# P divided by its row sums, and split into f16 halves, in two parts of eight heads each

## The chip, the cores and the metric

The kernel runs on one core of a Trainium2 chip. The metric is device time in microseconds for one execution. A core has five engines that run their own instruction streams and meet only at semaphores: TensorE (PE; its weight loads are shown as PEld), VectorE (DVE), ScalarE (ACT), GpSimd (POOL) and SyncE (SP, which here only issues DMAs). Within an engine instructions go in order.

## What is computed

The reference takes x, 64 batches of 64 positions by 512, and a condition of 64 by 512, and applies four residual layers one after the other: attention with a condition-dependent normalization, a linear resampling of the channels at places given by the condition, a GRU over the 64 positions and a coupled oscillator over the same positions. The change touches the first alone:

```python
xn = _rms_norm(x, g_norm) * (1.0 + scale) + shift      # scale, shift from the condition
q, k, v = split(xn @ W_qkv)                             # 16 heads of 32
q, k = _rms_norm(q, g_q), _rms_norm(k, g_k)
logits = einsum('bhqd,bhkd->bhqk', q, k) * 32 ** -0.5
attn = softmax(logits, axis=-1)
o = einsum('bhqk,bhkd->bhqd', attn, v)                  # heads joined to 512
x = x + o + o @ W_out
```

## The kernel before

The kernel has two stages. `recurrences` (GRU and oscillator, 64 steps in order) takes the time from about 640 us on and is not touched. `attention_and_sampling` fills the first 640 us. It works on pairs of batches: a pair is 2 x 64 = 128 tokens, one per partition, and there are 32 pairs, n = 0 to 31. The last four have the names N3, N2, N1 and N0.

The order of the work is written out by hand as a software pipeline. Each engine has a function `slot(pair, i)`, called for i = 0 to 30, in which `pair(d)` is the pair i + d. Pair i is projected in slot i (`project`, L1163), its scores and its softmax come in slot i + 1, `mix` (attention times V, L1241), the output projection (`proj`, L1253) and the residual in slot i + 2, and the resampling (`sample`, L1205) in slot i + 3. Since every engine takes its list in order, a late operation holds all that is behind it on its engine. The last pairs are written out after the loop.

All large products are made of f16 halves: a value is kept as its f16 rounding ("high") and the rest ("low"), and three products of halves are added. So for P (the attention weights) of pair p, with all 16 heads in `S` (128 x 1024, f32), the steps are, before:

- ScalarE, `exps`: 16 exponentials of 64 columns, one per head, each also summing its row into a column of `den` (two ahead of `high_o`, fourteen behind `guess`). For pairs 0 and 1, and for the last two, one Exp of the whole and a sum on VectorE take their place.
- VectorE, `invert_sum` (L860): the reciprocal of `den`, 128 x 16.
- POOL, `norm_p` (L432): `S` times it, 128 x 1024 in one instruction.
- ScalarE, `high_halves`: `S` to f16, last in its slot, behind `high_v` (V's high part) and `high_wr` (a piece of the weights of the GRU).
- POOL, `low_halves` (L437): the rest, to f16.
- SP, `turn_p` (L317): one transposing DMA takes both halves to `PT`, which `mix` reads in the next slot. It is the first entry in SP's slot. Behind it stand the load of x for three pairs on (L285), and the loads of `rows` (L289) and others.

For the last two pairs (N1, N0) TensorE turns P (`turn_p`, L1173), and there are no halves on POOL.

Around it, in a slot:

- VectorE, in order: `scale_x` (L779, waits for `keep_rs` on ScalarE), a one-hot build of 128 x 512 f16 (`build`, L795), `low_qk` (L771 and L774, which release `scores`, L1187), three builds, `sums_qk` (L817), `least` (L841), `sums_qk`, `means` (L804, writes `ms`), two builds, `low_o` (L881, writes the low part of `oT`, for which `proj` waits), `newton` (L809, L811, L813), `scale_qk` (L824), two builds, `invert_sum` (L860), `residual` (L888), `low_v` (L830), `weigh_taps` (L863), `low_wr` (L909, in slots 4 to 27), `weigh_taps`.
- POOL, in order: `modulate` of the next pair (L453, two instructions, waits for `scale_x`), `add_taps` twice (L425, L428), `low_x1` (L447, two), `low_x` (L460), `norm_p`, `low_halves`.
- TensorE, in order: `turn_qk` (L1141), `project` 0, `scores`, `project` 1, `mix`, `project` 2, `proj`, `sample`, `turn_x` (L1262, L1264).

At the end of slot 3 VectorE also makes some seeds (`seeds`, L983 to L988). Nearly all activations go through one helper and have its line, L515, in the profile.

Of the kernel before, what the change touches and what calls it, by code (L numbers as in the profile page):

```python
# [5 lines left out]
ALU = mybir.AluOpType  # L6
# [99 lines left out]
def attention_and_sampling(nc, sems, ctx, block, banks, S_, x2_done, x2_first, ts_, first4, XR, condT, ident, Wx, later, x, cond, W_emb, b_emb, g_norm,  # L106
# [23 lines left out]
    def sem(name):  # L130
        return sems.enter_context(nc.semaphore(name))
# [110 lines left out]
    wr_in = [sem(f"wr_in{k}") for k in range(2)]  # L242
    ph_done, pl_done, pt_in = sem("ph_done"), sem("pl_done"), sem("pt_in")
    wih_out = [sem(f"wih_out{u}") for u in range(2)]
# [37 lines left out]
    def _(sp):  # L282
# [31 lines left out]
        def turn_p(p):  # L314
            sp.wait_ge(pl_done, p.n + 1)
            need(sp, mix_done, p.n)
            sp.dma_start_transpose(PT[:, :, :, :].rearrange("p i j n -> p (i j) n"), halves.rearrange("p i s k -> p (i s k)"))\  # L317
                .then_inc(pt_in, 16)
# [64 lines left out]
    def _(pool):  # L383
# [46 lines left out]
        def norm_p(p):  # L430
            pool.wait_ge(rden_done, p.n + 1)
            nc.gpsimd.tensor_tensor(S[:, :, :], S[:, :, :], rden[:, :].unsqueeze(2).broadcast_to([PART, HEADS, T]), ALU.mult)\  # L432
                .then_inc(p_done, 1)

        def low_halves(p):
            pool.wait_ge(ph_done, p.n + 1)
            nc.gpsimd.tensor_tensor(halves[:, 1, :, :], S[:, :, :], halves[:, 0, :, :], ALU.subtract).then_inc(pl_done, 1)  # L437

# [74 lines left out]
    def _(act):  # L513
# [76 lines left out]

        def high_halves(p):
            act.wait_ge(p_done, p.n + 1)
            need(act, pt_in, p.n * 16)
            a(halves[:, 0, :, :], S[:, :, :]).then_inc(ph_done, 1)

# [5 lines left out]
        def exps(p, lo, hi):  # L601
            act.wait_ge(mn_done, p.n + 1)
            need(act, pl_done, p.n)
            for s in range(lo, hi):
                e = a(S[:, s, :], psB[:, s // 8, s % 8 * T:(s % 8 + 1) * T], ACT.Exp, scale=-1.0, bias=mn[:, s:s + 1],
                      accum_out=den[:, s:s + 1])
            if hi == HEADS:
                e.then_inc(exp_done, 1)
# [40 lines left out]
        def slot(pair, i):  # L649
# [36 lines left out]
            if p := pair(-1):  # L686
                if p.n > 1:
                    exps(p, 2, HEADS)
                else:
                    exps_at_once(p)  # L690
# [7 lines left out]
            if p := pair(-1):  # L698
                high_halves(p)

# [60 lines left out]
    def _(dve):  # L761
# [81 lines left out]
        def subtract_least(p):  # L843
            dve.wait_ge(mn_done, p.n + 1)
            if p.n == N0.n:
                dve.wait_ge(p_T, 1)
            else:
                need(dve, pl_done, p.n)
            v.tensor_tensor(S[:, :, :], psB[:, :, :].rearrange("p h (s k) -> p (h s) k", k=T),
                            mn[:, :].unsqueeze(2).broadcast_to([PART, HEADS, T]), ALU.subtract).then_inc(sub_done, 1)  # L850
# [5 lines left out]

        def invert_sum(p):
            dve.wait_ge(exp_done, p.n + 1)
            need(dve, p_done, p.n)
            v.reciprocal(rden[:, :], den[:, :]).then_inc(rden_done, 1)  # L860

# [128 lines left out]
        def slot(pair, i):  # L990
# [38 lines left out]
            if i == 0:  # L1029
                low_cp(0)  # L1030
            if tap:
                build(tap, 1, (2, 3))
            if p := pair(-1):
                if p.n < 2:
                    sum_p(p)
                invert_sum(p)
            if p := pair(-2):
# [57 lines left out]
        sum_p(N1)  # L1095
        invert_sum(N1)
        residual(N2)
# [6 lines left out]
        sum_p(N0)  # L1104
        invert_sum(N0)
        low_o(N1)
# [23 lines left out]
    def _(pe):  # L1130
# [36 lines left out]
        def turn_p(p):  # L1167
            pe.wait_ge(p_done, p.n + 1)
            need(pe, qk_ready, NP)
# [723 lines left out]
```

## Time and profile before

| | us |
|---|---|
| median of three runs | 1564.39 (1557.45 to 1566.65) |
| the profiled execution | 1563.98 |
| its span, first to last instruction | 1562.2 |
| steady slots of the first stage, from 107.45 to 545.40 | 437.95 |
| busy in the span: TensorE, VectorE, ScalarE, POOL | 1497.6, 1363.3, 942.4, 750.1 |

Times in rows are from the span's start. L12 is line 12 of the kernel before. A row of a timeline gives start, duration, engine, line, operation, output and inputs by the program's names, shape, count and, in brackets, how long the engine had been idle before and what released it; a tile shown as `front`, `room`, `first` or `x` can be another buffer laid over it (`halves` lies in `front`, the one-hot matrices in `room`).

### The profile page before, as it was taken

To read this page: it belongs to the slowest core of one execution; us is meant where nothing else is said; L and a number is where in the kernel's file an instruction comes from. 1 tells how busy PE (TensorE), PEld (TensorE's weight loads), DVE (VectorE), ACT (ScalarE), POOL (GpSimd) and SP (SyncE) were. 2 spreads that over 40 slices of the span, in tenths; PEclk is the share of its full clock that TensorE was granted. 3 is DMA by queue.
4 is the path that set the end of the run, shared out by engine and by line. 5 is a ranking of instruction groups with operands and counts; after the bars stand their busy time and mean duration, and the time that the engine had idled before them with its cause. 6 is when DMAs were issued, how large, how long until landed. Compare 5 with 4: busy or idle time off the path is not lost.

```text
span 1562.2 us, 95585 instructions
## 1 busy us (share of the span) xinstructions
PE 1497.6 (96%) x42219; PEld 1327.1 (85%) x42219; DVE 1363.3 (87%) x3259; ACT 942.4 (60%) x2854; POOL 750.1 (48%) x887
## 2 busy tenths in 40 slices
PE   6899999999999999899999999999999999999995
PEld 3467776666667767899999999999999999999995
DVE  7889889888888889498888989988999889988997
ACT  6667777767777764355555555555555555555553
POOL 2566666666666665443433343433434343434331
PEclk8999999999999999999999999999999999999996
DMA  6333333444444434000000000000000000000000
GB/s 226 57 81 95 88 84 83 96 101 100 103 109 100 83 65 130 10 12 15 15 13 14 15 15 13 13 15 15 14 13 15 15 15 13 13 15 14 14 13 15
DMA packets 169054, 75.56 MB, mean 48 GB/s; under 512 B 139768, under 2 KB 154272, under 8 KB 168640
## 3 DMA queue, kind: packets, MB, share of 16 engines
q1 hardware_dynamic: 168544, 69.44, 19.4%
q8 instruction: 331, 5.42, 1.5%
q14 instruction: 83, 0.68, 0.1%
q10 hardware_dynamic: 96, 0.02, 0.0%
HBM read 33.71 MB, written 11.60 MB: 29 GB/s over the span
## 4 chain that ended last, share of the span: by engine, by line
PE 82%; DVE 5%; ACT 4%; issue 3%; POOL 3%; DMA 2%; ACTq 0%; POOLq 0%; DVEq 0%
PE psB L1472 34%; PE psA L1501 15%; PE psQ L1163 10%; PE psA L1506 7%; PE psQ L1205 6%; PE psO L1253 4%; DMA PT<-front 2%; ACT S L515 2%; PE psO L1241 2%; PE psB L1187 1%; PE psA L1141 1%; POOL S L432 1%; POOL front L437 1%; ACT front L515 1%; DVE room L795 1%
## 5 line engine op out<-in xcount | busy, mean ns | idle before, releaser
L1472 PE MATMUL psB<-first,Wx 128*128 128x64 f16 x9216 | 293.5, 194 | 5.5 <-POOL first L1784 3.8
L1501 PE MATMUL psA<-ts,Cp 128*128 128x64 f16 x8160 | 283.8, 194 | 10.3 <-ACT ts L1539 10.0
L1472 PE MATMUL psB<-first,Whh 128*128 128x64 f16 x9072 | 286.4, 193 | 0.8
L1472 PEld LDWEIGHTS psB<-first,Wx 128*128 128x128 f16 x9216 | 280.7, 98 | 6.7 <-POOL first L1784 3.9
L1163 PE MATMUL psQ<-Wx,front 128*128 128x512 f16 x1152 | 269.4, 384 | 6.3 <-DVE front L970 4.1
L1472 PEld LDWEIGHTS psB<-first,Whh 128*128 128x128 f16 x9072 | 273.8, 98 | 1.6 <-issue 1.6
L1539 ACT ACTIVATE ts<-qst 128x256 f16<-128x256 f32 x192 | 80.1, 417 | 313.9 <-DVE qst L1643 313.9
L1501 PEld LDWEIGHTS psA<-ts,Cp 128*128 128x128 f16 x8160 | 258.7, 99 | 11.5 <-ACT ts L1539 11.0
L1163 PEld LDWEIGHTS psQ<-Wx,front 128*128 128x128 f16 x1152 | 108.8, 99 | 126.7 <-issue 8.1
L1780 POOL TENSOR_TENSOR en<-rz,dn 128x256 f32<-128x256 f32 x64 | 46.8, 731 | 255.8 <-issue 255.6
L1506 PE MATMUL psA<-ts,Cp 128*128 128x64 f16 x4080 | 163.4, 194 | 0.7 <-issue 0.2
L795 DVE TENSOR_SCALAR room<-rows,lidx 128x512 f16<-128x512 f16 x256 | 158.0, 659 | 0.2 <-issue 0.2
L1506 PEld LDWEIGHTS psA<-ts,Cp 128*128 128x128 f16 x4080 | 138.6, 99 | 1.4 <-issue 1.2
L432 POOL TENSOR_TENSOR S<-S,rden 128x1024 f32<-128x1024 f32 x32 | 61.0, 1905 | 157.6 <-DVE rden L860 157.6
L1670 DVE TENSOR_TENSOR ts<-psA,ts 128x256 f16<-128x256 f32 x255 | 107.1, 420 | 31.7 <-ACT psA L1539 26.3
L515 ACT ACTIVATE S<-psB,mn 128x64 f32<-128x64 f32 x448 | 133.2, 338 | 0.6 <-DVE mn L841 0.4
L1643 DVE SCALAR_TENSOR_TENSOR rest<-cub,psQ 128x256 f32<-128x256 f32 x256 | 106.3, 415 | 7.0 <-DVE cub L1674 0.5
L1780 POOL TENSOR_TENSOR V<-X3b,first 128x256 f32<-128x256 f32 x64 | 47.0, 735 | 134.1 <-DVE first L1764 133.9
L1205 PE MATMUL psQ<-x,room 128*128 128x128 f16 x1856 | 108.5, 219 | 0.0
L1643 DVE SCALAR_TENSOR_TENSOR psO<-qst,psO 128x256 f32<-128x256 f32 x256 | 106.5, 416 | 0.0
L1205 PEld LDWEIGHTS psQ<-x,room 128*128 128x128 f16 x1856 | 104.9, 98 | 0.2
L515 ACT ACTIVATION_READ_ACCUMULATOR S<-psB,mn 128x1 f32 x448 | 104.0, 232 | 0.0
(201 smaller groups left out, 3001.0 us busy)
## 6 DMA issues: line engine op xcount, KB each, us to landing
front<-in_x SPq DMA_DIRECT2D x32, 256.0 KB, 4.6
rows<-rows_dram SPq DMA_DIRECT2D x64, 128.0 KB, 3.1
out<-ot SPq DMA_DIRECT2D x512, 16.0 KB, 1.8
x<-x SPq DMA_DIRECT2D x29, 224.0 KB
Whh<-in_L_cond_W_qkv SPq DMA_DIRECT2D x12, 256.0 KB, 7.2
room<-in_L_cond_W_hh SPq DMA_DIRECT2D x12, 256.0 KB, 2.7
room<-in_L_cond_W_ih SPq DMA_DIRECT2D x12, 256.0 KB, 2.8
wih_dram<-room SPq DMA_DIRECT2D x12, 256.0 KB, 3.2
```

What stands on the lines that cost most here:

```text
L432: nc.gpsimd.tensor_tensor(S[:, :, :], S[:, :, :], rden[:, :].unsqueeze(2).broadcast_to([PART, HEADS, T]), ALU.mult)\
L515: return nc.scalar.activation(out, in_, f, **k)
L795: e = v.tensor_scalar(E_of(p, b)[:, k, :], rows[b][:, :], lidx[:, k:k + 1], None, ALU.is_equal)
L1163: last = mm(psQ[:, n, :], xn[p.u][:, i, c, :], Wqkv[:, j, c, n * D:(n + 1) * D], start=(c == 0 and t == 0), stop=(c == KC - 1 and t == 2))
L1205: last = mm(o[:, m, :, :], E_of(p, b)[:, c, m * PART:(m + 1) * PART], x1_of(p)[:, :, i, c, b, :], start=(c == 0 and i == 0), stop=(c == KC ...
L1472: last = mm(o, W_[:, i, c, g * PART:(g + 1) * PART], src[:, j, c, :], start=False, stop=False, skip_group_check=True)
L1501: mm(psF[:, s % 2, m, :], Cp[:, i, c, m * PART:(m + 1) * PART], ts_[:, 0, c, :], start=(c == 0 and m == 0 and i == 0), stop=False, skip_gr ...
L1506: last = mm(psF[:, s % 2, m, :], Cp[:, 0, c, m * PART:(m + 1) * PART], ts_[:, 1, c, :], start=False, stop=(c == KC - 1), skip_group_check= ...
L1539: return nc.scalar.activation(out, in_, f, **k)
L1643: return v.scalar_tensor_tensor(out=flat(out), in0=flat(in0), scalar=scalar, in1=flat(in1), op0=ALU.mult, op1=op1)
L1670: v.tensor_tensor(ts_[:, 1, :, :], th, ts_[:, 0, :, :], ALU.subtract).then_inc(S["ts_ready"], 1)
L1780: return nc.gpsimd.tensor_tensor(flat(out), flat(in0), flat(in1), op)
```

## The change

P's division and its split are made in two parts, heads 0 to 7 and heads 8 to 15. The eighth exponential (s = 7) now signals `exp_half`. VectorE makes the first reciprocal (128 x 8) right after `scale_qk`, ahead of the last two builds, and the second where the whole one was. POOL multiplies the two parts in two instructions and then makes the two low parts in two. ScalarE makes the first high part after the sixteenth exponential and ahead of `high_v`, and the second at the end of the slot. The transposing DMA is one as before, and waits for both. For pairs 0 and 1 and for the last two, which have no exponentials by head, both parts start from the end of the whole, one after the other; `rden_done`, `p_done`, `ph_done` and `pl_done` count twice per pair, and all that waits for them is adjusted.

```diff
--- before.py
+++ after.py
@@ -240,7 +240,7 @@
     cp_in, wo_in, wo_plus, wo_hi, wo_lo, cT_done, cp_hi, cp_lo, wr_hi, wr_lo = (
         sem(n) for n in ("cp_in", "wo_in", "wo_plus", "wo_hi", "wo_lo", "cT_done", "cp_hi", "cp_lo", "wr_hi", "wr_lo"))
     wr_in = [sem(f"wr_in{k}") for k in range(2)]
-    ph_done, pl_done, pt_in = sem("ph_done"), sem("pl_done"), sem("pt_in")
+    ph_done, pl_done, pt_in, exp_half = sem("ph_done"), sem("pl_done"), sem("pt_in"), sem("exp_half")
     wih_out = [sem(f"wih_out{u}") for u in range(2)]
 
     def turned_coupling():
@@ -312,7 +312,7 @@
             sp.dma_start(stage[k % 2], wr_source(k)).then_inc(wr_in[k % 2], 16)
 
         def turn_p(p):
-            sp.wait_ge(pl_done, p.n + 1)
+            sp.wait_ge(pl_done, p.n * 2 + 2)
             need(sp, mix_done, p.n)
             sp.dma_start_transpose(PT[:, :, :, :].rearrange("p i j n -> p (i j) n"), halves.rearrange("p i s k -> p (i s k)"))\
                 .then_inc(pt_in, 16)
@@ -428,13 +428,16 @@
             nc.gpsimd.tensor_tensor(r, r, us, ALU.add).then_inc(x2_done, 1)
 
         def norm_p(p):
-            pool.wait_ge(rden_done, p.n + 1)
-            nc.gpsimd.tensor_tensor(S[:, :, :], S[:, :, :], rden[:, :].unsqueeze(2).broadcast_to([PART, HEADS, T]), ALU.mult)\
-                .then_inc(p_done, 1)
+            for h in range(2):
+                pool.wait_ge(rden_done, p.n * 2 + h + 1)
+                part = S[:, 8 * h:8 * h + 8, :]
+                nc.gpsimd.tensor_tensor(part, part, rden[:, 8 * h:8 * h + 8].unsqueeze(2).broadcast_to([PART, HEADS // 2, T]), ALU.mult)\
+                    .then_inc(p_done, 1)
 
         def low_halves(p):
-            pool.wait_ge(ph_done, p.n + 1)
-            nc.gpsimd.tensor_tensor(halves[:, 1, :, :], S[:, :, :], halves[:, 0, :, :], ALU.subtract).then_inc(pl_done, 1)
+            for h in range(2):
+                pool.wait_ge(ph_done, p.n * 2 + h + 1)
+                nc.gpsimd.tensor_tensor(halves[:, 1, 8 * h:8 * h + 8, :], S[:, 8 * h:8 * h + 8, :], halves[:, 0, 8 * h:8 * h + 8, :], ALU.subtract).then_inc(pl_done, 1)
 
         def low_x1(p):
             x1 = x1_of(p)
@@ -588,10 +591,10 @@
             need(act, mix_done, p.n - 1)
             a(Vt[p.u][:, 0, :], psQ[:, 2, :]).then_inc(v_hi, 1)
 
-        def high_halves(p):
-            act.wait_ge(p_done, p.n + 1)
+        def high_halves(p, h):
+            act.wait_ge(p_done, p.n * 2 + h + 1)
             need(act, pt_in, p.n * 16)
-            a(halves[:, 0, :, :], S[:, :, :]).then_inc(ph_done, 1)
+            a(halves[:, 0, 8 * h:8 * h + 8, :], S[:, 8 * h:8 * h + 8, :]).then_inc(ph_done, 1)
 
         def high_p(p, h):
             act.wait_ge(p_T, p.n - N2.n)
@@ -600,10 +603,12 @@
 
         def exps(p, lo, hi):
             act.wait_ge(mn_done, p.n + 1)
-            need(act, pl_done, p.n)
+            need(act, pl_done, p.n * 2)
             for s in range(lo, hi):
                 e = a(S[:, s, :], psB[:, s // 8, s % 8 * T:(s % 8 + 1) * T], ACT.Exp, scale=-1.0, bias=mn[:, s:s + 1],
                       accum_out=den[:, s:s + 1])
+                if s == HEADS // 2 - 1:
+                    e.then_inc(exp_half, 1)
             if hi == HEADS:
                 e.then_inc(exp_done, 1)
 
@@ -686,6 +691,7 @@
             if p := pair(-1):
                 if p.n > 1:
                     exps(p, 2, HEADS)
+                    high_halves(p, 0)
                 else:
                     exps_at_once(p)
             if i == 1:
@@ -696,7 +702,9 @@
             if 0 <= i - WR_FROM < WR_PIECES:
                 high_wr(i - WR_FROM)
             if p := pair(-1):
-                high_halves(p)
+                if p.n < 2:
+                    high_halves(p, 0)
+                high_halves(p, 1)
 
         act.wait_ge(cond_T, 1)
         a(condT[:, :, :], psC).then_inc(cond_kept, 1)
@@ -845,7 +853,7 @@
             if p.n == N0.n:
                 dve.wait_ge(p_T, 1)
             else:
-                need(dve, pl_done, p.n)
+                need(dve, pl_done, p.n * 2)
             v.tensor_tensor(S[:, :, :], psB[:, :, :].rearrange("p h (s k) -> p (h s) k", k=T),
                             mn[:, :].unsqueeze(2).broadcast_to([PART, HEADS, T]), ALU.subtract).then_inc(sub_done, 1)
 
@@ -854,10 +862,13 @@
             v.tensor_reduce(den[:, :], S[:, :, :], AX.X, ALU.add).then_inc(den_done, 1)
             dve.wait_ge(den_done, short(p))
 
-        def invert_sum(p):
-            dve.wait_ge(exp_done, p.n + 1)
-            need(dve, p_done, p.n)
-            v.reciprocal(rden[:, :], den[:, :]).then_inc(rden_done, 1)
+        def invert_sum(p, h):
+            if h == 0 and p.n in range(2, N1.n):
+                dve.wait_ge(exp_half, p.n - 1)
+            else:
+                dve.wait_ge(exp_done, p.n + 1)
+            need(dve, p_done, p.n * 2)
+            v.reciprocal(rden[:, 8 * h:8 * h + 8], den[:, 8 * h:8 * h + 8]).then_inc(rden_done, 1)
 
         def weigh(p, b, ts):
             return v.tensor_tensor(um[b][:, :, :, ts].rearrange("p c v t -> p (c v) t"),
@@ -1028,12 +1039,15 @@
             scale_qk(qk)
             if i == 0:
                 low_cp(0)
+            if (p := pair(-1)) and p.n > 1:
+                invert_sum(p, 0)
             if tap:
                 build(tap, 1, (2, 3))
             if p := pair(-1):
                 if p.n < 2:
                     sum_p(p)
-                invert_sum(p)
+                    invert_sum(p, 0)
+                invert_sum(p, 1)
             if p := pair(-2):
                 residual(p)
             low_v(qk)
@@ -1093,7 +1107,8 @@
         low_qk(N0, 0)
         low_qk(N0, 1)
         sum_p(N1)
-        invert_sum(N1)
+        invert_sum(N1, 0)
+        invert_sum(N1, 1)
         residual(N2)
         low_v(N0)
         least(N0)
@@ -1102,7 +1117,8 @@
         low_p(N1, 0)
         low_p(N1, 1)
         sum_p(N0)
-        invert_sum(N0)
+        invert_sum(N0, 0)
+        invert_sum(N0, 1)
         low_o(N1)
         weigh_taps(N3, 1)
         build(N2, 0, range(KC))
@@ -1165,7 +1181,7 @@
             last.then_inc(qkv_done, 1)
 
         def turn_p(p):
-            pe.wait_ge(p_done, p.n + 1)
+            pe.wait_ge(p_done, p.n * 2 + 2)
             need(pe, qk_ready, NP)
             if p.n == N0.n:
                 pe.wait_ge(pt_ready, 1)
```

## Rows read from the trace of the kernel before

**Rows 1.** The page: busy time of each engine, share of the span, instructions

```profile
PE 1497.6 (96%) x42219; PEld 1327.1 (85%) x42219; DVE 1363.3 (87%) x3259; ACT 942.4 (60%) x2854; POOL 750.1 (48%) x887
```

**Rows 2.** Windows: length, busy of each engine (instructions), granted clock, DMA, GB/s

```profile
107.45:545.40 437.95, 427.06 (x8474) 306.50 (x8473) 387.10 (x672) 324.10 (x1199) 290.58 (x265) 1.00 0.41 95
252.24:269.94 17.70, 17.60 (x356) 12.75 (x355) 15.00 (x29) 13.50 (x50) 11.27 (x11) 1.00 0.38 92
161.46:179.64 18.18, 17.76 (x356) 12.68 (x355) 16.98 (x29) 13.59 (x50) 12.81 (x12) 1.00 0.39 90
233.80:252.24 18.44, 17.97 (x355) 12.77 (x354) 17.40 (x29) 13.55 (x51) 12.94 (x12) 1.00 0.38 87
```

**Rows 3.** Waits of TensorE, 80 to 585 us: us in total, times, longest

```profile
PE psO L1241 <- DMA PT<-front: 3.8, 5, 1.0
PE psO L1241 <- issue: 1.9, 6, 0.6
PE psQ L1163 <- issue: 2.1, 2, 1.1
```

**Rows 4.** Timeline of TensorE, one slot: start us, us, instruction [idle before <-releaser]

```profile
165.01 0.97 PE L1187 MATMUL psB<-first 32*64 32x64 f16 x96
...
168.61 1.20 PE L1241 MATMUL psO<-PT,Vt 64*32 64x64 f16 x96
...
172.82 2.85 PE L1253 MATMUL psO<-oT,Wo 128*128 128x128 f16 x48 [0.32 <-DVE oT L881]
```

**Rows 5.** Timeline of VectorE and POOL, middle of the same slot

```profile
170.14 0.54 DVE L804 TENSOR_SCALAR ms<-ss 128x33 f32<-128x33 f32 x1
...
170.59 1.57 DVE L795 TENSOR_SCALAR room<-rows,lidx 128x512 f16<-128x512 f16 x2
...
169.04 1.59 POOL L447 TENSOR_TENSOR x<-XR,x 128x256 f16<-128x256 f32 x2
...
170.60 1.15 POOL L460 TENSOR_TENSOR front<-front 128x512 f16<-128x512 f32 x1
```

**Rows 6.** Timeline of POOL, starts of three slots

```profile
158.22 1.91 POOL L432 TENSOR_TENSOR S<-S,rden 128x1024 f32<-128x1024 f32 x1 [5.08 <-DVE rden L860]
161.29 2.14 POOL L437 TENSOR_TENSOR front<-S,front 128x1024 f16<-128x1024 f32 x1 [1.17 <-ACT front L515]
163.38 1.10 POOL L453 TENSOR_TENSOR front<-front,modA 128x512 f32<-128x512 f32 x1
...
236.01 1.10 POOL L453 TENSOR_TENSOR front<-front,modA 128x512 f32<-128x512 f32 x1
...
253.52 1.09 POOL L453 TENSOR_TENSOR front<-front,modA 128x512 f32<-128x512 f32 x1
```

**Rows 7.** Timeline of VectorE, both ends of the slot at 161.46

```profile
157.88 0.26 DVE L860 RECIPROCAL rden<-den 128x16 f32<-128x16 f32 x1 [1.19 <-ACT S L515]
...
160.42 0.69 DVE L909 SCALAR_TENSOR_TENSOR Whh<-room,Whh 128x512 f16<-128x512 f32 x1
...
161.97 0.69 DVE L779 TENSOR_TENSOR front<-psB,rsB 128x512 f32<-128x512 f32 x1 [0.17 <-ACT rsB L515]
...
173.36 1.29 DVE L824 TENSOR_TENSOR qn<-psQ,rs 128x512 f32<-128x512 f32 x2
...
175.39 0.25 DVE L860 RECIPROCAL rden<-den 128x16 f32<-128x16 f32 x1 [0.22 <-ACT S L515]
```

**Rows 8.** Groups of POOL, 80 to 585 us: count, busy us, mean ns

```profile
L453 POOL TENSOR_TENSOR front<-front,modB 128x512 f32<-128x512 f32 x27 | 28.3, 1049 | 2.1
```

**Rows 9.** Timeline of VectorE and POOL around 88 us

```profile
88.19 1.41 DVE L983 TENSOR_TENSOR brz<-vT 128x8 f32<-128x8 f32 x1
...
87.44 2.14 POOL L437 TENSOR_TENSOR front<-S,front 128x1024 f16<-128x1024 f32 x1 [1.17 <-ACT front L515]
```

**Rows 10.** Timeline of TensorE, the mix of pair 1

```profile
77.27 0.55 PE L1241 MATMUL psO<-PT,Vt 64*32 64x64 f16 x48 [1.58 <-DMA PT<-front]
```

**Rows 11.** The tile PT, 60 to 640 us: its DMAs from issue to landing

```profile
DMA to landing us min/median/max: 4.3/4.7/6.1
```

## What the change will do to the time

> **What bounds the kernel now.** I read the page first: TensorE is busy 96% of the span [rows 1]. The change touches the first 640 us only, so I cut the steady part of that stage into its slots (one slot per pair of batches). A slot starts with the transposes of q and k (L1141). From 107.45 to 545.40 us there are 24 (8474 matmuls at 356 in a slot), in 437.95 us, 18.25 each; TensorE is at full clock throughout. The slot at 252.24 took 17.70 us with TensorE busy for 17.60 of it: that is the floor. The slots at 161.46 and 233.80 took 18.18 and 18.44 [rows 2]. So all that the 24 slots hold above the floor is 437.95 - 24 x 17.70 = 13.2 us. Adding the slots before them, the change cannot be worth much over 15 us.
>
> The waits of TensorE between 80 and 585 us say what part is the transposing DMA: 3.8 us, in 5 slots of 28; 1.9 us stand in front of the same line with nothing named, 2.1 us inside the projections [rows 3]. The larger rest is short waits on VectorE, of which the one ahead of the output projection is seen in slot 161.46: L1253 waits there for `oT` (L881) [rows 4]. It comes 0.48 late, which is all of 18.18 less 17.70.
>
> Why is that wait there in one slot and not in the next? The middle of that slot answers it [rows 5]. One-hot builds (L795) and the small `ms` (L804) do not run while a POOL instruction runs: the `ms` at 170.14 ends 0.05 behind L447; the two builds at 170.59 end at 172.16, 0.41 after L460 (171.75), of which 0.15 is for the first and the rest for the second. Only then comes `low_o` (L881), and at 172.82 the output projection. So the time at which POOL starts its chain for the slot (modulate, L453) sets TensorE's loss at mid-slot: 163.38, 1.92 into the slot, gave 18.18, 1.28 gave 17.70, 2.21 gave 18.44 [rows 2, 6].
>
> **The change, part by part.** Times below are relative to the start of the following slot, here 179.64, the end of slot 161.46 (161.46 + 18.18). POOL's rows are [rows 6], VectorE's [rows 7].
>
> Sizes. Half a normalization is 128x512 f32 with one operand repeated along the row, the form of L453's second row: 1.05 us; half of the low parts has the form of L460, 1.15 to 1.16 us [rows 8, 5]. Two halves cost 2.10 and 2.32 against 1.91 and 2.14 whole, less 0.04 of overlap each: POOL works 0.3 us more in a slot of which it is busy for 12.81 of 18.18 [rows 2]. The copy of the whole to f16 on ScalarE fits between the end of L432 (160.13) and the start of L437 (161.29), 1.16 with two handovers of about 0.05. Half of it I take as 0.62, a little over the half, since a fixed part stays. The extra reciprocal is 0.25 on VectorE.
>
> 1. First reciprocal. It stands behind `scale_qk` (L824), which ends at 173.36 + 1.29 = 174.65, at -4.99. The eighth exponential is long done, so it ends at -4.80; POOL starts 0.08 later (158.14 to 158.22) and holds -4.75 to -3.70.
> 2. Today's reciprocal at 175.39 (-4.25) was released by ScalarE, so the last exponential ends at -4.3, and only the last two stand beside the first product. ScalarE then waits to -3.64 and copies to -3.02, and `Vt`'s high part ends at about -2.4 instead of -3.7. `low_v` on VectorE comes two residuals behind the second reciprocal, at -2.2: no cost. These are what is queued behind the new wait on ScalarE: `high_v`, then `high_wr`, which ends at -1.9, also before L909 wants it at -1.1; the second copy follows to -1.4.
> 3. The two builds that followed L824 now stand behind the first reciprocal. One starts before POOL, the other is held to -3.70 and ends at -3.55, 0.15 behind. The second reciprocal ends at R = -3.37. In this slot the single one ended at 175.64 = -4.00; in the slot before, at 158.14 = -3.32. The gap that VectorE had there is used up.
> 4. POOL then runs without a gap: second product to R + 1.13, first low part to R + 2.24, second low part R + 2.20 to R + 3.36 = 0.0. L437 used to end at 163.43, 1.97 into the slot. SP therefore issues the transposing DMA some 1.9 us earlier. Issue to landing is 6.1 us at most [rows 11]; `mix` starts at 168.61, 7.15 in [rows 4]: the 3.8 us of waits go. The load of x, behind it on SP, also goes out earlier; it is for three slots on, so worth nothing.
> 5. What it collides with. `low_wr` (L909, two operands in SBUF) starts 2.28 behind a reciprocal's end (160.42 - 158.14). Today POOL is idle there (L432 ended at 160.13, L437 starts at 161.29). Now the second low part has started 0.08 us before it. No row shows L909 against POOL. The nearest: L983, also two SBUF operands, of only 8 columns, took 1.41 us at 88.19, beside the L437 that ends at 89.58, and ended with it [rows 9]. So the bounds for L909's delay are 0 (it gets in first; a new neighbour on POOL cannot make it earlier) and 1.08 us (held from R + 2.28 to R + 3.36); the row nearest in kind says held, and I take 1.0. Then L909, with its 0.6 behind that, ends at +0.6, the second `weigh` at +1.2, `scale_x` starts at 1.1 instead of 0.51 (161.97), and modulate at 1.87.
>
> 1.87 is where slot 161.46 had it (1.92). The low parts no longer delay it, but VectorE, held by the same low parts, does. And the next slot ends as this one does, so every slot becomes like 161.46: 18.18 us, no DMA wait. `low_qk` would end at 3.35 and `scores` started at 3.55 (165.01, [rows 4]), so nothing is added there. What ends last instead of the DMA is `oT` (L881), 0.48 per slot.
>
> The Trainium skill (SBUF — State Buffer, "Who interferes with whom") states the rule that speaks against this change: VectorE and GpSimd share a port pair, a VectorE instruction with two SBUF inputs contends with a GpSimd one that reads SBUF, and the second to issue fully blocks. L983 and the builds agree with it. By that rule L909 is held and the sum is the one below; without it (L909 takes part of no conflict) the first rival holds.
>
> Sum for the 24 slots: 24 x 18.18 = 436.3. The unnamed stalls at `mix` fall ahead of the wait on `oT` and vanish in it; of the 2.1 us inside the projections I keep 1.5. That is 437.8 against 437.95: -0.1.
>
> Before them, ScalarE has one Exp of the whole and everything is serial. A normalization with its copy and low parts takes 5.2 us, as from 158.22 to 163.43 [rows 6]; in halves it is 1.05 + 1.05, 1.16 after a copy that is hidden, and 1.16: 4.3. Twice, for pairs 0 and 1, this is on the chain (the second is the 1.58 us wait for `PT` at 77.27 [rows 10]): -1.8. L983, which held VectorE at 88.19 for the low parts, is free: -1.2. At the end, pairs 30 and 31 issue both halves back to back: +0.15 in each of the two, +0.3. Sum -0.1 - 1.8 - 1.2 + 0.3 = -2.8. The profiled execution took 1563.98 us (1.8 around its span), the median of the three is 0.4 higher: 1561.2.
>
> **Rivals.**
> First: VectorE gets in ahead of the second low part, since the margin in step 5 is 0.08 us and comes from durations of other lines. Then L909 is on time, the low part starts about 0.6 later and ends at +0.6, before the build at 1.1; modulate starts at 1.3 as in the slot at 252.24. Every slot is near the floor: 24 x 17.70 + 1.9 + 2.1 [rows 2, 3] = 428.8, -9.1; with -2.7 for the rest, 1552. For it: the slot at 252.24 is so, with the same work in it. Against it: L983 and the builds of [rows 5] began after a POOL instruction and were held.
>
> Second, slower: both builds are held by the first product, or the released one takes longer, so R is -3.0 or later instead of -3.37. The mechanism is L795 behind POOL at -4.7; its price is the 0.35 us by which L909, `scale_x` and modulate are later. Modulate at 2.2 is slot 233.80: 24 x 18.44 + 1.5 = 444.1, +6.1, less 2.7: 1567.5. It decides from R = -3.2 on, where `low_qk` passes 3.5. For it: VectorE is the fuller engine then (17.40 of 18.44 us [rows 2]) and gets 0.25 us more.
>
> Third, the change does not do what it says: the DMA stays unhidden, because the halves are serial on POOL behind a late ScalarE. Steps 1 to 4 leave about 1 us before that, and it would cost only the 3.8 us of today: 1564. I give it little and count it to the forecast's side.
>
> **How the numbers follow.** Forecast (L909 held, DMA wait gone) 0.5, with its own range 1558 to 1565; first rival 0.26; second 0.24. The range goes to both rivals, whose unknown is the 0 to 1.08 us on L909: 1551 to 1569. A measurement of this kernel can tell about 1% (16 us) from no change. Faster by that needs more than the whole excess of 13.2: 0.04. Slower by that needs 0.65 us in each of the 24 slots, more than slot 233.80 has over the mean: 0.03. Within: 0.93.
>
> **What would show it.** L317 issued about 0.0 to 0.1 into the slot and no wait on `PT` ahead of L1241; L432 at 1.05 us and L437 at 1.16 us, 60 or more of each; L909 at about 1.7 us instead of 0.69; L779 at 1.1 into the slot; slots of 18.2 with L1253 waiting on L881; L983 at about 0.2. It is wrong if L909 stays at 0.69 (first rival), if `scores` (L1187) waits on L774 in most slots (second), or if modulate starts at another time than 1.9.

## The result, and the profile after

The changed kernel takes 1550.63 us, the median of 13 runs (1548.0 to 1558.34). The kernel before, run 13 times by now, takes 1559.94 (1557.45 to 1571.61). The ratio is 0.994 with a 95% interval of 0.9925 to 0.9955: 0.6% faster, where I had forecast 1561.2, 0.2% faster, and a range that ended at 1551. About 4 of the 10.6 us between 1561.2 and 1550.63 are not the change: the forecast was taken off one execution of 1563.98, which stands that far above the median of 13. Against that median the change was worth 9.3 us where I had said 2.8. Run again later beside other kernels it gave 0.9927 (0.9899 to 0.9956); one of those six executions ran at a granted clock of 0.63, took 2202 us and is left out.

First the stage that the change touches. The windows of the profile after: all 24 steady slots, and two neighbours (length, busy us of PE, PEld, DVE, ACT, POOL, then clock, DMA share, GB/s).

```profile
103.08:533.52 430.44, 426.48 (x8474) 304.56 (x8473) 416.01 (x697) 327.25 (x1223) 298.80 (x312) 1.00 0.40 97
...
246.55:264.43 17.88, 17.76 (x355) 12.68 (x354) 17.27 (x30) 13.50 (x51) 12.40 (x13) 1.00 0.37 91
...
264.43:282.42 17.99, 17.77 (x356) 12.69 (x354) 17.48 (x30) 13.82 (x51) 12.50 (x13) 1.00 0.43 91
```

The 24 slots went from 437.95 us [rows 2] to 430.44: -7.5. They no longer range from 17.69 to 19.11 (of the five near 19, three held a wait on the DMA and two a stall of TensorE with nothing named) but are of two kinds that take turns, 17.88 and 17.99. VectorE is busier by 29 us over the stretch, some 20 of them the time that `low_wr` takes longer. The slots ahead of them ended 4.4 us earlier (103.08 against 107.45), the two behind them took 34.9 us instead of 35.7. By the start of the part in which the last pairs are written out (581.09, now 568.41) that is 12.7 us. What follows, some 52 us of last pairs and then the recurrences, which hold none of the change, differs between profiles of any two kernels here by several us (981.1 us to the end of the span before, 977.8 after, 971.9 to 983.2 in the experiments), so the 16 us between the two spans is not the change's worth. The ratio is.

The waits of TensorE from 80 to 572 us, after, in answer to [rows 3]: this is the whole list (it leaves out waits of up to 0.15 us).

```profile
PE psO L1269 <- DVE oT L892: 0.4, 1, 0.4
```

`PT` is gone from it. What is left is seen when the timelines of one slot are laid side by side. The slot before ends and the next starts at 264.43. POOL after, in answer to [rows 6]:

```profile
259.63 1.04 POOL L434 TENSOR_TENSOR S<-S,rden 128x512 f32<-128x512 f32 x1 [3.08 <-DVE rden L871]
261.02 1.04 POOL L434 TENSOR_TENSOR S<-S,rden 128x512 f32<-128x512 f32 x1 [0.34 <-DVE rden L871]
262.02 2.28 POOL L440 TENSOR_TENSOR front<-S,front 128x512 f16<-128x512 f32 x2
266.12 1.09 POOL L456 TENSOR_TENSOR front<-front,modA 128x512 f32<-128x512 f32 x1 [1.82 <-DVE front L787]
```

VectorE after, the end of the same slot and the middle of the next, in answer to [rows 7] and [rows 5]:

```profile
263.33 1.52 DVE L920 SCALAR_TENSOR_TENSOR Whh<-room,Whh 128x512 f16<-128x512 f32 x1
264.76 0.68 DVE L874 TENSOR_TENSOR um<-psQ,WT 128x512 f32<-128x512 f32 x1
265.37 0.68 DVE L787 TENSOR_TENSOR front<-psB,rsB 128x512 f32<-128x512 f32 x1
...
273.12 0.34 DVE L812 TENSOR_SCALAR ms<-ss 128x33 f32<-128x33 f32 x1
273.38 1.57 DVE L803 TENSOR_SCALAR room<-rows,lidx 128x512 f16<-128x512 f16 x2
274.87 0.68 DVE L892 TENSOR_TENSOR oT<-psO,oT 128x512 f16<-128x512 f32 x1
```

SP's queue with the transposing DMA, and the output projection on TensorE:

```profile
264.32 1.66 SPq L317 DMA_TRANSPOSE PT<-front  x1
...
275.60 2.85 PE L1269 MATMUL psO<-oT,Wo 128*128 128x128 f16 x48
```

The low parts (L440, before L437) end at 264.30, 0.13 us before the slot starts, where the whole one ended 1.97 into it, and the DMA goes out at once, 7 us ahead of `mix`. But `low_wr` (L920, before L909) starts at 263.33, 0.20 after the second low part (263.13), and takes 1.52 us instead of 0.69. `weigh_taps` and `scale_x` (L787) follow it without a gap, and POOL, idle for 1.82 us, starts to modulate (L456) at 1.69 into the slot. Then at mid-slot `ms` and the two builds are held behind POOL, and L892 comes late for the output projection, which starts 11.07 or 11.17 us into the slot. Those are the 17.88 and 17.99.

The profile after also holds a slot that shows what this costs. `low_wr` exists in slots 4 to 27 only, so the slot at 533.52 is the first with none ahead of it. Its low parts stand as in the others, from 2.42 before its start:

```profile
533.52:551.21 17.69, 17.59 (x355) 12.76 (x354) 15.43 (x29) 13.05 (x50) 12.20 (x13) 1.00 0.28 63
...
531.10 2.28 POOL L440 TENSOR_TENSOR front<-S,front 128x512 f16<-128x512 f32 x2
...
534.80 1.09 POOL L456 TENSOR_TENSOR front<-front,modA 128x512 f32<-128x512 f32 x1 [1.42 <-DVE front L787]
...
544.41 2.84 PE L1269 MATMUL psO<-oT,Wo 128*128 128x128 f16 x48
```

Modulate starts at 1.28 there, the output projection at 10.89, and the slot takes 17.69. The same slot takes 17.69 in each experiment below that holds `low_wr` back in the slots before it (e4, e7, e8, e10).

### The profile page after: what moved, and what is told of

Read it like the earlier page. It is cut to its first block, busy times and chain, and to the rows that moved or that the text cites. A ratio compares the mean times of both kernels' runs of the same rounds, so it can differ in the third digit from the quotient of the medians.

```text
span 1546.2 us, 95769 instructions
## 1 busy us (share of the span) xinstructions
PE 1490.6 (96%) x42219; PEld 1321.0 (85%) x42219; DVE 1392.7 (90%) x3291; ACT 946.2 (61%) x2884; POOL 759.4 (49%) x949
## 3 DMA queue, kind: packets, MB, share of 16 engines
q1 hardware_dynamic: 168544, 69.44, 19.1%
## 4 chain that ended last, share of the span: by engine, by line
PE 89%; DVE 5%; issue 2%; POOL 1%; ACT 1%; DMA 0%; ACTq 0%; POOLq 0%; DVEq 0%
PE psB L1488 35%; PE psA L1517 15%; PE psQ L1179 13%; PE psA L1522 8%; PE psQ L1221 7%; PE psO L1269 5%; PE psA L1157 2%; PE psB L1203 2%; PE psO L1257 1%; DVE room L803 1%; PE psB L1278 1%; DVE ss L825 1%; ACT front L518 1%; DVE oT L892 1%; POOL S L434 0%
## 5 line engine op out<-in xcount | busy, mean ns | idle before, releaser
L803 DVE TENSOR_SCALAR room<-rows,lidx 128x512 f16<-128x512 f16 x256 | 182.2, 754 | 0.1
L434 POOL TENSOR_TENSOR S<-S,rden 128x512 f32<-128x512 f32 x64 | 66.6, 1043 | 122.1 <-DVE rden L871 122.1
```

What stands on the lines that cost most here:

```text
L803: e = v.tensor_scalar(E_of(p, b)[:, k, :], rows[b][:, :], lidx[:, k:k + 1], None, ALU.is_equal)
```

## The experiments

All ratios are to the kernel before, run beside each kernel. "24 slots" is the stretch from the fifth turn of q and k to the twenty-ninth, in the one profiled execution of each.

| kernel | ratio (95%) | 24 slots, us | usual slot, us |
|---|---|---|---|
| before | 1 | 437.95 | 17.7 to 19.1 |
| changed | 0.994 (0.9925 to 0.9955) | 430.44 | 17.88 / 17.99 |
| changed, again | 0.9927 (0.9899 to 0.9956) | 430.50 | the same |
| e1 | 0.9929 (0.9907 to 0.995) | 429.52 | 17.69 / 17.74 |
| e2 | 1.0003 (0.9983 to 1.0022) | 435.89 | 17.7 to 19.0 |
| e3 | 0.9905 (0.988 to 0.9931) | 426.99 | 17.69 / 17.73 |
| e3, again | 0.9931 (0.9905 to 0.9957) | 429.86 | 17.69 / 17.74 |
| e4 | 1.0085 (1.0058 to 1.0112) | 449.98 | 18.75 |
| e5 | 0.9988 (0.997 to 1.0007) | 434.17 | 17.7 to 19.1 |
| e7 | 0.9952 (0.9932 to 0.9972) | 433.40 | 17.69 / 18.25 |
| e8 | 0.9918 (0.9891 to 0.9944) | 428.76 | 17.69 / 17.85 |
| e9 | 0.9899 (0.9878 to 0.9919) | 428.26 | 17.69 / 17.74 |
| e10 | 0.9976 (0.9955 to 0.9997) | 438.20 | 18.25 |

**e1: `low_wr` moved to where POOL is idle.**

```diff
             newton(i + 2, cols)
+            if 0 <= i - WR_FROM < WR_PIECES:
+                low_wr(i - WR_FROM)
             scale_qk(qk)
...
             if tap:
                 weigh_taps(tap, 0)
-            if 0 <= i - WR_FROM < WR_PIECES:
-                low_wr(i - WR_FROM)
```

(and `high_wr` on ScalarE from behind `high_v` to ahead of the second `squares_qk`)

> The changed kernel with high_wr (ScalarE) moved ahead of the second squares and low_wr (L909's operation, VectorE) moved to between newton and scale_qk, where POOL is idle. Theory (what is left above 17.70 us per slot is low_wr held behind the second low part, by 0.84 us): low_wr takes 0.69 us again, modulate starts 1.3 us into the slot, the 24 slots take 17.7 each, 425 to 427 us instead of 430.4, and the kernel 5 to 6 us less than the changed one: about 1545, ratio to before about 0.9905. Rival (the wait of the output projection on oT comes from VectorE being fuller, wherever low_wr stands): no change from the changed kernel, 0.994.

VectorE of e1, ahead of the reciprocals and at the start of the slot at 463.05:

```profile
456.51 0.68 DVE L920 SCALAR_TENSOR_TENSOR room<-room 128x512 f16<-128x512 f32 x1
...
463.56 0.69 DVE L787 TENSOR_TENSOR front<-psB,rsB 128x512 f32<-128x512 f32 x1 [0.17 <-ACT rsB L518]
```

`low_wr` is 0.68 us again, `scale_x` waits for ScalarE and not for VectorE's own queue, and 19 of the 24 slots take 17.69 to 17.76. So, as in the slot at 533.52 of the changed kernel, the 0.24 us left per slot are the hold on `low_wr`. The total did not follow: two slots of 19.91 and 19.20 hold stalls of TensorE that the profile names nothing for:

```profile
PE psQ L1179 <- issue: 3.4, 2, 2.0
```

Each of the two begins within 1 us of a 16 KB packet of the instruction queue (at 163.22 and 253.76 us), and that packet came about 14 us behind the one before it. All nine stalls of over 1 us with nothing named, in the 24 slots of the thirteen profiles, begin within 2 us of a packet that came 12.7 us or more behind the last; in the changed kernel's two profiles, with 67 such packets as here, no interval is over 10.6 us and there is no such stall. Seventeen packets were as late as that, so eight of them brought none. I have not tested this as the cause. Without these two the slots would have summed to about 425.8.

**e2: the same move in the kernel before.**

> The kernel before with the same move of high_wr and low_wr. Theory (low_wr was never held in the kernel before, so its place costs nothing there): within 2 us of before, ratio 0.999 to 1.001; the waits on PT stay. Rival (low_wr's place ahead of the second weigh_taps costs by itself): 5 us less, 0.997.

No difference, as expected: 1.0003, and there are still waits on the DMA. `low_wr` was not held before (0.67 to 0.70 us in all its slots), and its place as such costs nothing that these runs can tell.

```profile
PE psO L1241 <- DMA PT<-front: 2.3, 3, 1.0
```

**e3: two parts, neither beside the exponentials.**

```diff
-            if (p := pair(-1)) and p.n > 1:
-                invert_sum(p, 0)
             if tap:
                 build(tap, 1, (2, 3))
             if p := pair(-1):
                 if p.n < 2:
                     sum_p(p)
-                    invert_sum(p, 0)
+                invert_sum(p, 0)
                 invert_sum(p, 1)
...
                 high_wr(i - WR_FROM)
             if p := pair(-1):
-                if p.n < 2:
-                    high_halves(p, 0)
+                high_halves(p, 0)
                 high_halves(p, 1)
```

(and without the `high_halves(p, 0)` behind the exponentials)

> The changed kernel with both reciprocals after the sixteenth exponential and both f16 copies at the end of the slot: two parts, but none beside the exponentials. Theory (the gain comes from POOL finishing the low parts early, and the pipelining of the parts gives about 1 us of the 1.9): POOL ends about 0.35 or 1.3 us into a slot, slots alternate between 17.7 and 18.3, the DMA wait is mostly gone; 1 to 4 us slower than the changed kernel, ratio to before 0.995 to 0.997. Rival (the overlap with the exponentials is what pays): as before, 1.000.

Both were wrong. e3 was not slower than the changed kernel; its ratio came out lower, with intervals that just overlap. POOL and VectorE of e3, the slot that starts at 442.67:

```profile
440.89 2.73 POOL L440 TENSOR_TENSOR front<-S,front 128x512 f16<-128x512 f32 x2 [0.24 <-ACT front L518]
443.95 1.09 POOL L456 TENSOR_TENSOR front<-front,modA 128x512 f32<-128x512 f32 x1 [0.32 <-DVE front L785]
```

```profile
441.90 0.70 DVE L918 SCALAR_TENSOR_TENSOR room<-room 128x512 f16<-128x512 f32 x1
442.53 0.68 DVE L872 TENSOR_TENSOR um<-psQ,WT 128x512 f32<-128x512 f32 x1
443.18 0.69 DVE L785 TENSOR_TENSOR front<-psB,rsB 128x512 f32<-128x512 f32 x1
```

Here the low parts start 0.3 us later behind the second reciprocal, since the copies stand behind `high_wr` on ScalarE. `low_wr` begins at 441.90, while the first low part still runs (it ends at 442.06), is not slower for it (0.70), and it is the second low part that waits: the two take 2.73 us instead of 2.28. POOL has time for that; VectorE has not. Modulate starts at 1.28 and the slots are at the floor.

**e3 again, and the changed kernel again, on one chip.**

> The changed kernel once more, to stand beside the next two on the same chip: ratio to before 0.994, its 24 slots 430 us in the profile, all between 17.88 and 17.99.

> e3 once more. Theory (in the changed kernel the half that runs beside the exponentials costs, since it lines the second low part up with low_wr): 3 to 6 us faster than the changed kernel on the same chip, 24 slots of about 427 us. Rival (the two differ by chance): within 2 us of it.

The changed kernel repeated its slots to 0.1 us (430.50). e3 did not repeat its total. Its slots were again 17.69 to 17.75 where nothing else happened, but 1.4 us of stalls in a projection and 1.6 us ahead of `mix`, with nothing named, made 429.86. Medians 1551.17 and 1551.74: no difference. A small stall can vanish in the wait on `oT`, which comes behind `mix`: in e10 below, a stall of 1.13 us in a projection made a slot of 18.99 out of one of 18.25, so 0.39 of it was covered. That does not account for the rest, since the changed kernel's two profiles had no stall to cover above 0.2 us. So the half that runs beside the exponentials is worth nothing that the times can tell; by the undisturbed slots it costs about 0.2 us each, through `low_wr`.

**e4: the low parts in one instruction.**

```diff
-            for h in range(2):
-                pool.wait_ge(ph_done, p.n * 2 + h + 1)
...
+            pool.wait_ge(ph_done, p.n * 2 + 2)
+            nc.gpsimd.tensor_tensor(halves[:, 1, :, :], S[:, :, :], halves[:, 0, :, :], ALU.subtract).then_inc(pl_done, 2)
```

> The changed kernel with the low parts in one POOL instruction of 2.14 us after both copies. Theory (a POOL instruction holds back VectorE's low_wr and builds for its whole length): the DMA is still issued by 0.8 us into the slot and no slot waits for PT, but low_wr is held for about 1.8 us, modulate starts at 2.4, and slots take 18.4 to 18.5: 24 of them 442 to 444, about 12 us more than the changed kernel, ratio to before 1.000 to 1.003. Rival (the early transposing DMA is what pays): as the changed kernel, 0.994.

This tells the theory from its rival most clearly. POOL and VectorE at the slot that starts at 444.75:

```profile
443.32 2.14 POOL L439 TENSOR_TENSOR front<-S,front 128x1024 f16<-128x1024 f32 x1 [0.94 <-ACT front L517]
447.29 1.08 POOL L455 TENSOR_TENSOR front<-front,modA 128x512 f32<-128x512 f32 x1 [1.83 <-DVE front L786]
```

```profile
443.62 2.38 DVE L919 SCALAR_TENSOR_TENSOR room<-room 128x512 f16<-128x512 f32 x1
```

The low parts end at 445.46, 0.71 into the slot: ahead of the 1.3 to 2.3 of the kernel before, and no wait on the DMA is left. Yet the kernel is 0.85% slower than before. `low_wr`, sent 0.30 us behind its start, is held until it ends (2.38 us), modulate starts at 2.54, and TensorE waits twice in nearly every slot:

```profile
PE psB L1202 <- DVE first L781: 9.5, 24, 0.4
PE psO L1268 <- DVE oT L891: 9.4, 23, 0.4
```

I had expected 442 to 444 us and got 449.98: with modulate at 2.54 a second wait (`scores` on `low_qk`) comes on top, 0.40 per slot (the first line), and I had not counted it. In e10, with modulate at 2.02, it is not there.

**e5: the product whole, copies and low parts in two, none early.**

> As e3 (both parts after the exponentials), but the product with 1/sum in one POOL instruction of 1.91 us; copies and low parts in two. Theory (what pays is that POOL is done by the time VectorE's first build and scale_x want it, and the copy cannot start before the whole product): low parts end at about 2 us into the slot as before, the alternation of 17.7 and 18.4 and part of the DMA waits stay; ratio to before 0.996 to 1.000. Rival (short POOL instructions at the start of the slot, which hold VectorE for 1.1 us at most, pay by themselves): as e3, 0.990 to 0.992.

0.9988: the alternation stays (slots of 17.70 and 18.3), and so do waits on the DMA. Short low parts by themselves are worth little; with the product whole the low parts end at 1.36 to 2.1 us into a slot, with it in two at 0.4 to 1.0 (e3). That the copy and the low part can follow its first half is what brings the end forward.

```profile
PE psO L1251 <- DMA PT<-front: 2.6, 3, 1.2
```

**e7: e3 with the first copy ahead of `high_wr`.**

```diff
+            if (p := pair(-1)) and p.n > 1:
+                high_halves(p, 0)
             if 0 <= i - WR_FROM < WR_PIECES:
                 high_wr(i - WR_FROM)
```

> As e3, but with the first copy on ScalarE ahead of high_wr, so that it ends 0.65 us earlier. In e3 low_wr began 0.04 us before the second low part and made that one wait (1.61 us long). Theory (who comes first at the boundary decides): the low parts come 0.3 us earlier, low_wr then begins behind the second one in the slots where the exponentials end late and is held about 0.9 us; these slots take 18.3 to 18.5, the others 17.7: 432 to 440 us for the 24 slots and ratio to before 0.994 to 0.999, slower than e3 although ScalarE and POOL are earlier. Rival (an earlier end of the low parts is never worse): as e3, 0.990, or faster.

An earlier copy makes it slower, as expected: 433.40 us, slots of 17.69 and 18.25 in turn, and one of 20.00 with a stall of 2.1 us with nothing named. POOL and VectorE of two neighbouring slot ends:

```profile
303.56 2.27 POOL L440 TENSOR_TENSOR front<-S,front 128x512 f16<-128x512 f32 x2
...
321.62 2.74 POOL L440 TENSOR_TENSOR front<-S,front 128x512 f16<-128x512 f32 x2
```

```profile
304.86 1.52 DVE L921 SCALAR_TENSOR_TENSOR Whh<-room,Whh 128x512 f16<-128x512 f32 x1
...
322.46 0.87 DVE L921 SCALAR_TENSOR_TENSOR room<-room 128x512 f16<-128x512 f32 x1
```

In the first, `low_wr` comes 0.18 us behind the start of the second low part (about 304.68) and is held; in the second it comes while the first low part still runs (until about 322.78) and the second low part pays. Half a microsecond lies between the two here; over all runs the change falls between an operation that started level with the second low part and went first (e3 again) and one that started 0.12 us behind it and was held.

**e8: the changed kernel with `low_wr` ahead of the first `weigh_taps`.**

```diff
+            if 0 <= i - WR_FROM < WR_PIECES:
+                low_wr(i - WR_FROM)
             if tap:
                 weigh_taps(tap, 0)
-            if 0 <= i - WR_FROM < WR_PIECES:
-                low_wr(i - WR_FROM)
```

> The changed kernel with low_wr ahead of the first weigh_taps on VectorE, so that it begins while the first low part runs and gets the port at the boundary, before the second. Theory: it ends at 2.85 us behind the second reciprocal instead of 3.91, the second low part shows 1.6 us instead of 1.16, scale_x starts at 0.5, modulate at 1.3, slots take 17.7 (24 of them 425 to 428): 5 to 6 us less than the changed kernel, ratio to before about 0.990. Rival (low_wr is held by both low parts, or the loss is elsewhere): 0.994 or worse.

POOL and VectorE of e8:

```profile
265.27 2.73 POOL L440 TENSOR_TENSOR front<-S,front 128x512 f16<-128x512 f32 x2
268.85 1.09 POOL L456 TENSOR_TENSOR front<-front,modA 128x512 f32<-128x512 f32 x1 [0.85 <-DVE front L787]
```

```profile
265.96 1.01 DVE L920 SCALAR_TENSOR_TENSOR Whh<-room,Whh 128x512 f16<-128x512 f32 x1
```

`low_wr`, sent 0.6 us earlier, waits for the rest of the first low part only and ends at 266.97, 2.79 behind the reciprocal, against 3.91. Usual slots fall to 17.69 and 17.85. The sum, 428.76, is 1.7 us under the changed kernel and not 5: every second slot is still 0.1 to 0.2 late, since the second reciprocal, and all behind it, comes up to 0.42 us later than in the changed kernel, and there are 1.7 us of stalls with nothing named. 0.9918 (0.9891 to 0.9944) overlaps both comparisons of the changed kernel: no difference shown in the time.

**e9: e3 with e1's move.**

> e3 (both parts after the exponentials) with low_wr and high_wr moved as in e1. Theory (e3's slots are at TensorE's floor of 17.7 already, low_wr is not held there): no change from e3 within 2 us, ratio to before 0.989 to 0.992. Rival (low_wr ahead of scale_qk frees VectorE in any version): 3 or more us less than e3.

0.9899 (0.9878 to 0.9919), the lowest ratio of all, and its slots sum to within 1.3 us of e3's first ones: both are at the floor, and moving `low_wr` adds nothing to e3 that shows, as expected. It is ahead of the changed kernel's first comparison by more than the intervals, not of its second.

**e10: the first reciprocal behind the builds.**

```diff
+            if tap:
+                build(tap, 1, (2, 3))
             if (p := pair(-1)) and p.n > 1:
                 invert_sum(p, 0)
-            if tap:
-                build(tap, 1, (2, 3))
```

> The changed kernel with the first reciprocal behind the last two builds instead of ahead of them; the first copy stays ahead of high_v. Theory (what counts is where the second low part stands when low_wr comes): the builds are no longer held, but the first copy ends later, so high_v and low_v are 0.5 us later, low_wr comes about 0.1 us behind the second low part and is held as in the changed kernel, and modulate starts at 2.0 or later: slots of 18.1 to 18.3, 24 of them 434 to 440 us, ratio to before 0.996 to 1.000, so slower than both others. Rival (the holding of the builds is the cost of the changed kernel): 17.7 to 17.8 per slot, as e3.

The builds are not held any more, and it is slower: 438.20 us, 18.25 a slot. So freeing the builds is worth nothing here; they are held ahead of the slot at 533.52 of the changed kernel too, and it takes 17.69. POOL and VectorE of e10, the slot that starts at 306.74:

```profile
304.46 2.47 POOL L440 TENSOR_TENSOR front<-S,front 128x512 f16<-128x512 f32 x2
308.76 1.09 POOL L456 TENSOR_TENSOR front<-front,modA 128x512 f32<-128x512 f32 x1 [1.83 <-DVE front L787]
```

```profile
304.69 0.69 DVE L838 TENSOR_TENSOR Vt<-psQ,Vt 128x512 f16<-128x512 f32 x1 [0.48 <-ACT Vt L518]
305.30 0.68 DVE L874 TENSOR_TENSOR um<-psQ,WT 128x512 f32<-128x512 f32 x1
305.89 1.58 DVE L920 SCALAR_TENSOR_TENSOR Whh<-room,Whh 128x512 f16<-128x512 f32 x1
```

`low_v` now waits 0.48 us for ScalarE, which had to make the first copy before `Vt`; `low_wr` is held as in the changed kernel, but later, and modulate starts at 2.02. That gives the loss a fourth point: modulate at 1.28, 1.69, 2.02 and 2.54 gave slots of 17.70, about 17.93, 18.25 and 18.75, the last with the wait of `scores` in it.

## Why the prediction was wrong

In the steady slots the mechanism stood and its sizes did not, and they all erred the same way.

Right: the product's half at 1.04 us (1.05 said), the low half at 1.16; POOL's order from the second reciprocal on (low parts to 3.36 us behind it, in all 24 slots); the DMA at -0.1 us and its wait gone; `low_wr` held by the second low part, to 3.91 us behind the reciprocal where I had 3.97 (2.28 + 1.0 + 0.69); VectorE in place of the low parts as what delays modulate; `oT` as the last wait, and `scores` untouched. The seeds' L983 (now L994) took 0.16 us instead of 1.41.

Wrong, the term of the sum "24 x 18.18 = 436.3". It rested on modulate at 1.87, "where slot 161.46 had it". It came at 1.69, by which the prediction itself was to be called wrong ("if modulate starts at another time than 1.9"). The reciprocal of 8 columns takes 0.19, not the 0.25 of 16: the first ended at -4.88 instead of -4.80, the build held behind the product at -3.61 instead of -3.55, and the second reciprocal at -3.50 and not -3.37. With the 0.06 by which `low_wr` was held less, that is the 0.18. And the 18.18 was measured with modulate at 1.92, not 1.87. Between 1.7 and 2.0 the slot follows modulate about one to one (below that less: 1.28 to 1.69 costs 0.24), so 0.23 us there made 0.24 per slot: 17.94 against 18.18, 5.8 us over 24 slots. e1 and the slot at 533.52 show that what is left above 17.7 is the held `low_wr`, as the prediction had it; its effect was sized at 0.48 per slot and measured 0.24.

Wrong, "of the 2.1 us inside the projections I keep 1.5". The changed kernel showed none in either profile. Stalls with nothing named came and went from one kernel to the next (0 to 3.5 us over the 24 slots), e3's two profiles differ in them by 2 us, and I had taken one profile's worth as fixed. 1.5 us.

The term for the slots ahead, -3.0, was -4.4 in the first profile; over the ten profiles with the product in two the first of the 24 slots starts at 102.9 to 107.3, 105.1 in the mean; over the three without it (before, e2, e5) at 107.4 to 109.5, 108.8 in the mean. So it is about -3.7, and its size was nearly right, but not its working: the 1.58 us wait for `PT` at the mix of pair 1, which I counted as gone, is gone in the first profile after and 1.49 us in the second. Which part gave the rest is open. The two slots behind the 24 gained 0.8, for which I had no term. The last pairs, where I had said +0.3 for the halves back to back, took TensorE 51.4 us after and 51.95 before, and 51.35 to 51.95 over the three kernels with the product whole: no cost can be told.

The sum of the terms: -5.8, -1.5, -1.4, -0.8 and -0.8 are what the first stage did beyond my -2.8 (some 13 us in the pair of profiles, of which the ratio bears out 7 to 12). I had also said that a measurement here tells about 1% from no change; with 13 runs of each, 0.6% was clear of it.

The first rival, at 1552, came near the number by luck and another way: `low_wr` did not get in first in the changed kernel. It did in e3 and e8, and in e3 and every second slot of e8 gave the 17.7 us of this rival. The second rival (R at -3.0 or later) did not occur. It is e10 that is like it in time: 18.25 per slot.

By the rule of the Trainium skill (SBUF — State Buffer, "Who interferes with whom"), `low_wr` with two inputs in SBUF was to be blocked until the POOL instruction that had started first ended. The runs agree: it took 1.52 us when sent 0.20 us behind the start of a 1.16 us instruction, 2.38 us when sent 0.30 us behind the start of one of 2.14, and 0.69 where POOL was idle.

## What to carry to other kernels

Where VectorE and POOL hold each other back, read each in the other's timeline: an instruction on the engine with slack costs more the longer it is (e4 against the changed kernel), and an earlier end of it (e7 and e10 against e3) can be worse than a later one if it puts its last piece just ahead of something on the full engine. Cut what runs on the engine with slack into pieces, and send the operation of the full engine while the piece before is still running, so that it goes first at the boundary. And where a wait of 0.2 us per slot is removed from an engine that is 99% busy, one profile may not show it in the sum: of the 5.6 us that the changed kernel's 24 slots had above 17.7, e1, e3 (twice) and e9 gained 0.6 to 3.5, with 1.3 to 3.4 us of stalls with nothing named. Read it in the single slots.

## What the runs showed of the hardware that I had not expected

Who is first at a boundary: in e3 and e8 VectorE's operation was sent while the first of two POOL instructions ran, and it ran before the second, though POOL had that one ready; the second then took 1.61 us instead of 1.16. One sent 0.12 to 0.25 us after the second had started (changed kernel, e7, e10) was held to its end. And `low_wr` in e3, sent 0.16 us before the end of the first low part, showed no delay at all (0.70 us).
